# Dot attention's edge one-hots made during propagation, and the clip's lower bound taken within the weighing

## The reference

```python
# h = relu(layernorm(x)); each layer adds to x
# layer 0: ten propagation steps, h = initial value, w = 1/sqrt(deg_row*deg_col)
for _ in range(K):
    out = spmm(out) * BETA + h * ALPHA
# layer 1: graph attention over src -> dst (softmax by dst), tanh
# layer 2: dot attention
q = (embeds[rows] @ qW).reshape(e, HEADS, dh)
k = (embeds[cols] @ kW).reshape(e, HEADS, dh)
v = (embeds[cols] @ vW).reshape(e, HEADS, dh)
scores = jnp.clip(jnp.einsum('ehd,ehd->eh', q, k), -10.0, 10.0)
exp_s = jnp.exp(scores)
norms = jax.ops.segment_sum(exp_s, rows, num_segments=nvar)[rows]
w = exp_s / (norms + 1e-08)
res = jax.ops.segment_sum(w[:, :, None] * v, rows, num_segments=nvar).reshape(nvar, d)
# layer 3: messages x[src] @ W + b, mean over dst
```

## Time and profile before

| | us |
|---|---|
| three runs | 1624.86, 1625.02, 1630.6 |
| median of the runs | 1625.02 |
| the profiled execution, its own time | 1627.73 |
| its span, first to last instruction | 1625.9 |
| propagation's ten turns, from and to | 325 to 860 |
| dot attention's loop, from and to | 1249.5 to 1526.4 |
| VectorE busy in all | 1259.8 |
| TensorE busy in all | 1237.4 |

### The profile page before, as it was taken

How to read it: one execution, slowest core, us unless ns; L and a number is a source line. 1 busy time by engine, 2 the same in 40 slices (tenths; PEclk the granted TensorE clock), 3 DMA queues, 4 the chain that set the end, 5 groups by cost and what they waited for, 6 DMA issues and landing times. The chain is left out here.

```text
span 1625.9 us, 44876 instructions
## 1 busy us (share of the span) xinstructions
PE 1237.4 (76%) x18543; PEld 1174.0 (72%) x18544; DVE 1259.8 (77%) x2302; ACT 546.2 (34%) x1096; POOL 373.9 (23%) x211
## 2 busy tenths in 40 slices
PE   4767777399999999999994004888856888888468
PEld 3356767399899999999993004787755887888368
DVE  7888888766566565665667998999988999999733
ACT  0047777400000000000002873333335777777311
POOL 1400000000000000000001012888862665656300
PEclk6858777699999999999997556999997999999789
DMA  0012222375475565654563683555513444543293
GB/s 10 0 46 109 105 103 109 109 249 190 151 240 204 161 196 194 213 194 164 203 213 110 225 298 123 204 201 189 200 68 117 144 159 149 164 146 122 96 343 101
DMA packets 74936, 256.85 MB, mean 158 GB/s; under 512 B 17999, under 2 KB 19576, under 8 KB 74732
## 3 DMA queue, kind: packets, MB, share of 16 engines
q1 hardware_dynamic: 59996, 211.70, 38.6%
q10 hardware_dynamic: 14400, 40.97, 6.5%
q0 software_dynamic: 336, 1.20, 0.3%
HBM read 168.15 MB, written 85.68 MB: 156 GB/s over the span
## 5 line engine op out<-in xcount | busy, mean ns | idle before, releaser
L1248 PE MATMUL psum<-work,count 128*128 128x192 f16 x6250 | 521.4, 247 | 30.7 <-issue 30.7
L1248 PEld LDWEIGHTS psum<-work,count 128*128 128x128 f16 x6250 | 519.7, 98 | 32.5 <-issue 31.8
L1171 DVE SCALAR_TENSOR_TENSOR work<-psum,small,work 128x96 f32<-128x96 f32 x250 | 79.5, 318 | 177.4 <-PE psum L1248 177.3
L1585 PE MATMUL psum<-count 128*128 128x98 f16 x625 | 113.1, 209 | 134.5 <-DVE count L1632 98.2
L1852 PE MATMUL psum<-count 128*128 128x100 f16 (+1 forms) x1875 | 181.4, 207 | 44.5 <-DVE count L1941 30.7
L1852 PEld LDWEIGHTS psum<-count 128*128 128x128 f16 x1875 | 162.7, 98 | 55.3 <-issue 36.0
L929 ACT ACTIVATE work<-work 128x1248 f32<-128x1248 f32 (+1 forms) x6 | 7.2, 1203 | 576.9 <-DVE work L912 576.8
L1917 POOL TENSOR_TENSOR count<-count 128x1000 bf16<-128x1000 f32 (+1 forms) x75 | 160.8, 2143 | 122.0 <-ACT count L1901 122.0
L1624 POOL TENSOR_TENSOR count<-count 128x970 bf16<-128x970 f32 (+1 forms) x75 | 166.7, 2236 | 91.2 <-ACT count L1617 91.2
L1853 PE MATMUL psum<-count 128*128 128x100 f16 (+1 forms) x1875 | 180.8, 207 | 0.0
L1853 PEld LDWEIGHTS psum<-count 128*128 128x128 f16 x1875 | 164.4, 98 | 0.0
(11 more groups left out here) (286 smaller groups left out, 2695.7 us busy)
## 6 DMA issues: line engine op xcount, KB each, us to landing
x<-bucket_rows_by_src SPq DMA_DIRECT2D x100, 400.0 KB, 4.6
onehots_by_src<-x ACTq DMA_DIRECT2D x100, 400.0 KB, 4.3
count<-bucket_rows_by_dst SPq DMA_DIRECT2D x50, 800.0 KB, 4.4
count<-onehots_by_src SPq DMA_DIRECT2D x50, 800.0 KB, 4.3
count_f<-count SPq DMA_DIRECT2D x25, 800.0 KB, 6.8
count<-count_turned SPq DMA_DIRECT2D x25, 800.0 KB, 5.8
count<-count_f SPq DMA_DIRECT2D x17, 800.0 KB, 4.3
count_turned<-x SPq DMA_DIRECT2D x25, 416.0 KB, 2.4
```

Of the source, the lines that this page charges most:

```text
L1248: last = nc.tensor.matmul(bank[i % BANKS], count16[:, j, i * P:(i + 1) * P], y[par][:, j, :], start=(j == 0), stop=(j == TILES - 1))
L1585: nc.tensor.matmul(ps[:, at:at + GW], node_hot[SRC][t % 2][:, s, :], high[:, s, :], start=True, stop=False, skip_group_check=True)
```

## The change

All three one-hots of dot attention are now made in propagation. `NodeSpots` becomes `Spots`: 150 pieces instead of 100, of which each third one (1, 4, 7, ...) is an edge half of 13 or 12 tiles (1664 or 1536 columns), made by comparing a row 0..127 with node numbers that lie on the partitions. For that the source half of bucket_ids is loaded at the start of propagation (128 x 25 runs of 100 B). Node halves have four buffers instead of three; the edge halves have one, and each compare of them waits for the store of the one before. The fourth node buffer, the edge buffer and the numbers lie in the place of `y32`, so the update's passing value now has two small buffers of its own, and `y32` is written only in the last turn, before which VectorE waits for all stores. The pieces are spread over turns 0 to 8: after tiles 1 to 20, at five of each six places. Eleven semaphores of the first stage are cleared by GpSimd in the block before propagation and used again.

In dot attention `spot_edges` and the load of `cols` are gone; SyncE loads three one-hots for each s instead of two, the third after `scattered` of s-3. ScalarE makes two steps instead of three: Relu(10 - score), then Exp(10 - that), which is the upper bound alone; the lower bound is a maximum with exp(-10) (`least`, both scaled by 2 to the -6) within the weighing, which becomes a scalar_tensor_tensor: (weight max least) times v. Paths for graphs with more edges (`large`, `many`) change in the same way, and don't run here.

```diff
 propagate(), VectorE, the usual path
-                for turn in range(K_STEPS):
-                    for i in range(TILES):
-                        update(dve, turn * TILES + i, bank[i % BANKS], at_tile(i), y[1 - turn % 2])
-                        if i in SPOT_AFTER:
-                            spots.compare(dve, halves, turn * len(SPOT_AFTER) + SPOT_AFTER.index(i))
+                for turn in range(K_STEPS):
+                    if turn == LAST:
+                        spots.wait_stored(dve)
+                    for i in range(TILES):
+                        update(dve, turn * TILES + i, bank[i % BANKS], at_tile(i), y[1 - turn % 2], y32[:, i, :] if turn == LAST else passing[i % 2])
+                        q = 20 * turn + i - 1
+                        if turn < LAST and 1 <= i <= 20 and q % 6 < 5:
+                            spots.compare(dve, pieces, 5 * (q // 6) + q % 6)
...
 the pieces
-HALF_ROW = NPAD // 2
+HALF_ROW, HALF_TILES = NPAD // 2, ((0, 13), (13, TILES))
+NODE_HALVES, EDGE_HALVES = 4 * TILES, 2 * TILES
+PIECES, NODE_BUFFERS = NODE_HALVES + EDGE_HALVES, 4
...
+    def load_ids(self, sp, pieces, k, ids_dram):
+        ids = ids_dram[bass.ds(k, 1)].rearrange("k p t n -> (k p) t n")[:, :, SRC * TILES * 2:(SRC + 1) * TILES * 2]
+        sp.dma_start(pieces.ids.rearrange("p t s d -> p t (s d)"), ids).then_inc(self.ids_loaded, 16)
...
+    def compare_edges(self, dve, pieces, e):
+        s, half = divmod(e, 2)
+        t0, t1 = HALF_TILES[half]
+        if e == 0:
+            dve.wait_ge(self.counted, 1)
+            dve.wait_ge(self.ids_loaded, 16)
+        else:
+            dve.wait_ge(self.edges_stored, 16 * e)
+        shape = [P, t1 - t0, P // 2, 2]
+        self.nc.vector.tensor_tensor(pieces.edge[:, 0:(t1 - t0) * P].rearrange("p (t n d) -> p t n d", n=P // 2, d=2),
+                                     pieces.iota.rearrange("p (n d) -> p n d", d=2).unsqueeze(1).broadcast_to(shape),
+                                     pieces.ids[:, t0:t1, s, :].unsqueeze(2).broadcast_to(shape), ALU.is_equal).then_inc(self.made, 1)
...
 dot_attention(), SyncE
-                    for v, done in ((SRC, "q_done"), (DST, "v_done")):
+                    for v, done in ((SRC, "q_done"), (DST, "v_done"), (EDGE, "scattered")):
                         sp.wait_ge(S[done], (s - 2) * PER)
                         load_hot(sp, s, v)
...
 ScalarE
-                        nc.scalar.activation(below[0][:, 0:w], score[j % 2][:, 0:w], ACT.Relu, scale=-1.0, bias=m["small"][:, 590:591]).then_inc(S["capped"], 1)
+                        nc.scalar.activation(below[j % 2][:, 0:w], score[j % 2][:, 0:w], ACT.Relu, scale=-1.0, bias=m["small"][:, 590:591]).then_inc(S["capped"], 1)
                         act.wait_ge(S["capped"], j + 1)
-                        nc.scalar.activation(below[1][:, 0:w], below[0][:, 0:w], ACT.Relu, scale=-1.0, bias=twenty).then_inc(S["clipped"], 1)
-                        act.wait_ge(S["clipped"], j + 1)
-                        nc.scalar.activation(weight[j % 2][:, 0:w], below[1][:, 0:w], ACT.Exp, bias=exp_bias).then_inc(S["exped"], 1)
+                        nc.scalar.activation(weight[j % 2][:, 0:w], below[j % 2][:, 0:w], ACT.Exp, scale=-1.0, bias=exp_bias).then_inc(S["exped"], 1)
...
 VectorE
-                        if s + 1 < TILES:
-                            if t0 == GROUP:
-                                spot_edges(s + 1)
...
-                        nc.vector.tensor_tensor(heads(banks(value[i % 2], n, VW), VH), heads(group_of(4, n, VW), VH),
-                                                weight[i % 2][:, 0:n * HEADS].rearrange("p (b i) -> p b i", i=PER_BANK * HEADS).unsqueeze(3).broadcast_to([P, n // PER_BANK, PER_BANK * HEADS, VH]),
-                                                ALU.mult).then_inc(S["weighed"], 1)
+                        nc.vector.scalar_tensor_tensor(heads(banks(value[i % 2], n, VW), VH),
+                                                       weight[i % 2][:, 0:n * HEADS].rearrange("p (b i) -> p b i", i=PER_BANK * HEADS).unsqueeze(3).broadcast_to([P, n // PER_BANK, PER_BANK * HEADS, VH]),
+                                                       least, heads(group_of(4, n, VW), VH), ALU.max, ALU.mult).then_inc(S["weighed"], 1)
```

More of the change, by code:

```diff
@@ L933, in _, with spot_next_round @@
             scalar_after(act)
-def spot_next_round(nc, m, halves, row, hot, n):
+def spot_next_round(nc, m, pieces, k, ids_dram, by_src, hot_by_src):
     spots = m["spots"]
@@ L941, in _, with many @@
         def _(sp):
-            if_one(sp, m, None, lambda: spots.loads(sp, halves, row, n))
+            def many():
+                spots.load_ids(sp, pieces, k, ids_dram)
+                for n in range(NODE_HALVES):
+                    spots.load(sp, pieces, k, n, by_src)
+            if_one(sp, m, None, many)
         @block.vector
@@ L946, in many @@
             def many():
-                for i in range(n):
-                    spots.compare(dve, halves, i)
+                dve.sem_inc(spots.counted, 1)
+                for piece in range(PIECES):
+                    spots.compare(dve, pieces, piece)
             if_one(dve, m, None, many)
@@ L953, in many @@
             def many():
-                spots.stores(act, halves, hot, n)
-                spots.wait_stored(act, n)
+                spots.stores(act, pieces, hot_by_src)
+                spots.wait_stored(act)
             if_one(act, m, None, many)
@@ L1217, in _ @@
         def _(act):
-            spots.stores(act, halves, half_hot, HALVES)
+            spots.stores(act, pieces, hot_by_src)
         @block.tensor
@@ L1255, in large @@
             def large():
-                for i in range(HALVES):
-                    spots.compare(dve, halves, i)
+                for piece in range(PIECES):
+                    spots.compare(dve, pieces, piece)
+                spots.wait_stored(dve)
                 with dve.Fori(0, K_STEPS // 2) as kk:
```

156 lines of the change are left out of this document (85 added, 71 removed).

## The result

| | before | after |
|---|---|---|
| median of four runs, us (lowest to highest) | 1625.93 (1624.86 to 1630.6) | 1602.67 (1595.87 to 1606.92) |
| ratio of the times | | 0.9845, 95% interval 0.9815 to 0.9876 |
| the profiled execution | 1627.73 | 1606.92 |
| its span | 1625.9 | 1605.1 |

The kernel is 23.3 us faster, 1.5%. The prediction said 1583, with a range up to 1597: the sign is right, the size is not, and the time lies 5.7 us above the range. The profiled execution after is the slowest of its four, 4.25 us above the median.

What follows compares the result with a forecast made beforehand. TensorE was taken to bound propagation, VectorE dot attention's loop. 1627.7 - 42.2 + 0 + 1 - 0.5 = 1586.0 for an execution like the profiled one; less 2.7, 1583 for the median; range 1576 to 1597.

Steps and rivals of the forecast that it cites:

- Cost on the path: 0: Propagation: the 50 added edge-half pieces fit in VectorE's idle time of 177.3 us and cost 0 us.
- Rival C: Propagation gives back 10 to 15 us through the first edge half and edge-store waits at turn ends: 1596; chance 0.12.
- The dot loop: Dot attention: source tile from 10.81 to 9.05 us, 24 times, saves 42.2 us; bounds 39.8 to 43.7.
- The edits help each other: Dot attention: ScalarE's edit is worth more beside the one-hot move; new wait about 0.2 us, 0.55 with three steps.
- The weighing's new form: Dot attention's 75 weighings as scalar_tensor_tensor: taken as 0 us, bounds 0 to 5.4 us in all.
- B: Dot attention: each weighing costs 0.07 us more, all on the path: 1588; chance 0.16 together with F.
- F: Dot attention: removing the Relu does nothing because the cast holds the chain: 1589; chance 0.16 together with B.
- A: Dot attention: TensorE's floor of 8.66 us per source tile is reached, saving 51.6 us: 1574; chance 0.05.
- D: Dot attention: one-hot loads come late at 250 GB/s, period 9.8 us, gain only 24 us: 1602; chance 0.04.
- E: Propagation: the one edge buffer sets the pace, making the kernel slower than before, 1654 at a 9 us landing; chance 0.03.
- The first edge half: Start of propagation: waits for the node numbers' 3200 runs of 100 B; 1 us taken, bounds 0 and 4.
- Turn 9: End of propagation: without pieces, x is loaded earlier and its 0.98 us wait can go; gain taken as 0.5 us.

Runs made afterwards that it cites:

- quiet-ends run: Changed kernel with the same 150 pieces placed denser in even turns and ending after tile 14 in odd turns: 1617.07 us, ratio 0.9918.
- table of four above: First weighing to last add, us: one-hot in the loop 269.8 with three ScalarE steps, 262.4 with two; one-hot moved 242.2 with three, 229.6 with two.
- written-out kernel: Changed kernel with TensorE's loop of five passes over two propagation turns written out as ten turns: 1578.55 us, ratio 0.9693.
- two other kernels with the same propagation: Changed kernel with three ScalarE steps and the plain product kept, 1613.71 us; changed kernel without 22 edge one-hot loads in dot attention, 1602.63 us.
- three written-out kernels: TensorE's propagation loop written out: in the changed kernel 1578.55 us, in the kernel before 1618.28, in the changed kernel with node numbers loaded second 1579.71.

## Why the prediction was right or wrong

**Propagation, "Cost on the path: 0": this step failed.** Its cover was VectorE's idle time, and that held: the edge halves took 948 to 1026 ns, the wait for TensorE's sums fell from 177.3 to 132.7 us (130 had been named), VectorE's waits for stores and loads summed to 20.5 us and were caught up before the turns' ends. What the step left out is that the one-hots' transfers also use the DMA engines that bring TensorE its instructions, and that TensorE fetches some at each of four jumps, with nothing to do meanwhile; and that a longer pause is followed by more time at the lower clock. In the trace of before, pauses of 2.4 to 3.6 us stood at these places for anyone who asked why TensorE is busy 521 of 537 us; I read that number as "TensorE's stage" and didn't look at the rest. The pieces now stand behind nearly each tile up to 20, where they stood behind every second one up to 19, and their transfers are still running at the turn's end, 4 tiles later, where they had been over. Measured: +12.9 at the jumps and +1.4 in the tiles behind them; by TensorE's own rows, 8.3 of it standing still and some 6 the lower clock.

**Rival C had a number near the truth (1596) with the wrong mechanism.** It put 10 to 15 us on VectorE's waits for the edge store that reach a turn's end. None did in the changed kernel; the quiet-ends run shows what that looks like. The test that the prediction named for it, a wait of TensorE for y at the turns' ends, isn't in the trace of after; it appears, with 1.3 and 1.4 us at the end of turn 0, in two other executions of the same placement.

**The dot loop: right, a little too large.** 42.2 us were forecast and 24 x 1.70 = 40.8 measured by the period, 40.1 by the stretch. The period is 9.11, not 9.05, inside the stated 8.99 to 9.15. Step by step against the earlier trace rows: the one-hot's 1.73 went whole; in the full group 0.11 us of new wait and 0.05 in the add behind it appeared where 0.2 was forecast; in the half group only 0.16 of 0.29 went (1.36 to 1.20 us from multiplication to weighing). The last is the term that was too large. ScalarE's timeline of after says why:

```profile
1396.98 0.96 ACT L1943 COPY count<-psum 128x960 f32<-128x960 f32 x1 [0.65 <-PE psum L1905]
1397.84 1.03 ACT L1953 CAST count<-count 128x1000 f16<-128x1000 f32 x1
1398.76 0.32 ACT L1958 ACTIVATE work<-count,small 128x20 f32<-128x20 f32 x1
1399.11 0.31 ACT L1960 ACTIVATE count<-work 128x20 f32<-128x20 f32 x1
```

The copy of q now waits for TensorE's gathers and ends just when the cast could start; the cast runs at 1397.84, 0.23 us after the weighing's end at 1397.61, where it had 0.03 before, and holds the Relu and the Exp (to 1399.42) of the weighing at 1399.51. The prediction had this as its upper bound ("the cast before the Relu keeps its place and starts late") and took a value nearer to the lower one.

**The edits help each other:** right, by the table of four above. **The weighing's new form:** 0 us was taken, and it is 0 (means of L1988 by form; the earlier trace rows has 1.19 and 0.68 for the product that it replaced):

```profile
L1988 DVE SCALAR_TENSOR_TENSOR count<-count,psum 128x1000 f32<-128x1000 f32 x50 | 59.6, 1191 | 1.5 <-ACT count L1960 0.9
...
L1988 DVE SCALAR_TENSOR_TENSOR count<-count,psum 128x500 f32<-128x500 f32 x25 | 16.9, 674 | 2.1 <-ACT count L1960 1.1
```

So B falls. F falls by the ScalarE edit alone, which gained 7.4 us. A falls: the period stays 0.45 us above TensorE's 8.66. D, loads that come late, falls by the run without them, although they land in 7.0 us (median; 16.0 at most) instead of 4.3. E falls: the edge stores land in 8.3 us at most, and VectorE waited for them nine times, 10.3 us in all (up to 20.8 us in the other kernels of this placement).

**The first edge half:** 1 us was taken between 0 and 4. In the changed kernel the first piece starts at 338.98 after a wait of 3.33 us, and turn 0 lasted 51.95, so 0.4; in the written-out kernel 53.91, so 2.4; in the two other kernels with the same propagation 51.56 and 53.24. The term was of the right size. The load of 0.32 MB in runs of 100 B landed in 7.9 us; in the same kernel the loads of node halves, 0.41 MB each, landed in 5.9 us (median; 3.5 to 9.9). The Trainium skill (DMA: Bandwidth & Descriptors, Specifications) names 512 B as the least for line rate. The trace points the same way, since fewer bytes took longer than the median, but the 7.9 us lie within the range of the node loads, and no run here changes the length of the runs alone.

**Turn 9:** -0.5 was taken; the stretch is 0.8 shorter, of which 0.65 is the wait at x (0.98 to 0.33).

**The sum then.** For an execution like the profiled one 1586.0 was forecast, and 1606.9 measured, 20.9 more. The nine turns make 13.6 of it (14.6 where 1 was allowed), dot attention 2.1, turn 9 takes 0.3 off. The other 5.4 lie in the start (3.4), the stretch up to dot attention (0.7) and the last layer (1.3), which no edit touches, and aren't explained further; the last layer alone lasted between 99.4 and 100.9 us in the five kernels below that keep the loop.

## What to carry over

An engine at 97% of a stage isn't fully used: before calling a stage "its own", look for the rows in which it waits for nothing visible, and ask whether a loop of its program jumps there. Then look at the granted clock behind each pause: here it cost nearly as much again as the pauses' growth. Traffic that is free while the engine streams isn't free when that engine must fetch instructions; measured here, writing out a loop of five passes was worth 29 us in propagation and more than the edit under study lost. A step removed from a chain is worth most where the work that covered the chain is removed with it, so the pair has to be costed together.

## What was not expected of the hardware

- A jump back of TensorE costs 2.2 to 3.9 us of standing still with quiet DMA engines (12 jumps in three kernels: before, ScalarE's edit alone, quiet ends) and 3.8 to 6.2 with one-hots on them (16 jumps in four). In all 28, TensorE goes on 1.5 to 2.0 us after the end of its last instruction packet. With quiet engines that packet starts 0.2 to 0.5 us ahead of the end of the matmuls, with one-hots 0.4 to 2.6 behind it, and it takes 0.9 to 2.2 us in either case; what the traffic moves is the packet's start. That the fetch is queued behind data is read from these times. No run separates it from a fetch that is asked for later.
- The granted clock falls behind pauses, and the length of a pause alone doesn't say whether. It fell behind all 16 jumps with one-hots and behind 7 of the 12 quiet ones, among them one of 2.26 us, while it stayed up behind one of 3.15. After the pause that ends at 548.63 it stood at 0.50 until 554.5, and a tile took 2.93 us instead of 2.06; a part of that stretch (window: length, busy of the five engines, clock, DMA share, GB/s):

```profile
548.60:552.00 3.40, 3.37 (x22) 3.18 (x23) 0.00 (x0) 0.00 (x0) 0.00 (x0) 0.50 0.02 5
```

- Writing a loop out moves the fetches instead of only removing them: all three written-out kernels had a pause of 5 us in the last layer, under loads of 390 to 410 GB/s, that their originals didn't have. Why it falls there was not tested.
- GpSimd's low half of 1000 columns takes 3.46 us beside VectorE's edge one-hot and 1.95 without it (timeline of GpSimd before; the one-hot runs from 1398.85 to 1400.66):

```profile
1399.01 3.46 POOL L1917 TENSOR_TENSOR count<-count 128x1000 bf16<-128x1000 f32 x1 [2.27 <-ACT count L1901]
1403.63 1.95 POOL L1917 TENSOR_TENSOR count<-count 128x1000 bf16<-128x1000 f32 x1 [1.16 <-ACT count L1901]
```

They overlap for 1.65 us, and GpSimd takes 1.51 longer, nearly the whole overlap. So it goes for all 24 one-hots of the loop, 3.46 or 3.47 us each time; in the changed kernel, without them, no such step takes more than 2.10 us. That GpSimd stands still meanwhile is a reading of these times; no run isolates it. The mean for this form fell from 2680 to 2091 ns, off the path in both.
